# Another order of stages on all engines: score and value products apart on TensorE, the dense head and tail placed anew

## The chip, the cores and the metric

The kernel runs on one core of one Trainium2 chip. The metric is the device time of one launch in microseconds (us), median of three runs.

## The reference

The input is x, 2048 tokens of 128 features. It is layer-normalised to xn, and the output is x + dense(xn) + stack(xn).

- dense(xn): 16-head softmax attention over all 2048 tokens (head width 8, folded projections), then an output product with a bias.
- stack(xn): six layers. Each shifts half of the features by one token, projects to q, k, v (16 heads of 64), normalises each q and k row to unit length, applies gains and rotary tables, attends within a window of 32 tokens and the 32 before (mask, softmax over 64 keys), multiplies by Wo and adds the residual. Then a layer norm, a product up to 2 x 341 columns, a * gelu(gate), a product down to 128 and another residual.

## The kernel before

**Part A** (to about 790 us) is the dense attention: `tensor_a`, `scalar_a`, `vector_a`, `gpsimd_a`, `sync_a`. The change does not touch it. It leaves the unscaled dense result and its row sums in two scratch tensors in DRAM.

**Part B** is the stack: `tensor_b`, `scalar_b`, `vector_b`, `gpsimd_b`, `sync_b`. Its unit of work is a tile of 128 tokens, 16 tiles in each layer, 96 in all. The layer norm and the up and down products work on a chunk of four tiles, 24 chunks in all. Each engine runs one loop `for u in range(FIRST, LAST)`, a round, and a round calls each stage once, for the tile or chunk that is u minus a lag: `score(tile(u - 2))`. `chunk(x)` gives a chunk only for every fourth x. There is no scheduler: an engine works through its list in the order written, and waits at semaphores. The rounds of the engines are not in step; only the semaphores tie them.

The stages of a tile: `high_x` and `low_x` cut the input into two parts (ScalarE, GpSimd); `project(u, 0|1|2)` makes q, k and v, six products of 512 columns each (L1274 to L1276); `squares` (ScalarE, L710) and `square_sums` (VectorE, L982) give the row norms; `rotate_cos` (L1000) and `rotate_sin` (L1011, L1012) multiply out of PSUM; `rotated` (L639) and `normalise` (L647) on GpSimd add and scale; `turn` (L1300) transposes four heads' pairs, `turned_q` and `turned_k` (L732, L741, L744) copy them out; `score` (L1315, L1320) is 2 mask products and 128 recorded small ones; `maxima` (L1031), `exponentials` (L762), `prob_sums` (L1038), `prob_reciprocals` (L1045), `scale_probs` (L601) and `blocks` (L1023) are the softmax and its transpose; SyncE's `move_probs` (L464) and `shift_v` (L455, L456) lay out probabilities and v; `values` (L1337) is 128 recorded small products; `values_out` (L752), `output` (L1349) and `residual_1` (L1055) end the tile.

Each small product is one weight load and one matmul, so score is some 260 instructions of TensorE and values 256, where a projection is 12.

Every product writes to PSUM banks that a table, `BANKS`, fixes for even and odd tiles. A later user of a bank waits until the engine that empties it for the user before has signalled (`wait_free`); `bank_users` repeats TensorE's order to find who that is.

The dense result enters in `load_dense` (SyncE), `dense_norm` (VectorE, L1151: reciprocal of the row sums, then a product), `dense_output` (TensorE L1396, ScalarE L846) and `store_dense`, in four early rounds. It leaves in `load_dense_out`, `final_sum`, `finish` (L1405), `final_add`, `store_out` in late rounds.

Of the kernel before, what the change touches and what calls it, by code (L numbers as in the profile page):

```python
# [16 lines left out]
NT = T // P  # L17
CH = 512
NC = T // CH
# [9 lines left out]
DEPTH = 6  # L29
# [34 lines left out]

END = DEPTH * NT
CHUNKS = DEPTH * NC
FIRST, LAST = 0, END + 15
AHEAD = NT + 2
NPT = 8
NV = 4  # L70
# [29 lines left out]
def tile(x):  # L100
    return x if 0 <= x < END else None


def chunk(x):
    c, r = divmod(x - 3, 4)
    return c if r == 0 and 0 <= c < CHUNKS else None


def early(x):
    return x if 0 <= x < NC else None  # L110


def late(x):
    c = chunk(x)
    return c if c is not None and c >= CHUNKS - NC else None
# [1 line left out]


BANKS = {"q": ((4, 5), (4, 5)), "k": ((2, 3), (2, 3)), "v": ((0, 1), (4, 5)),
         "q_turn0": ((1,), (6,)), "q_turn1": ((6,), (7,)), "k_turn0": ((6,), (7,)),  # L120
         "k_turn1": ((0,), (1,)), "values": ((2, 3), (2, 3)), "output": ((6,), (6,)),
         "score": ((0, 1), (0, 1)), "mean": ((7,), (7,)), "var": ((4,), (4,)),
         "up0": ((4, 5), (4, 5)), "up1": ((2, 3), (2, 3)), "up2": ((6, 7), (6, 7)),
         "down": ((7,), (7,)), "att": ((7,), (7,)), "finish": ((7,), (7,))}
OUT = {"q": "q_out", "k": "k_out", "v": "v_out", "q_turn0": "qT_out0", "q_turn1": "qT_out1", "k_turn0": "kT_out0", "k_turn1": "kT_out1",
       "values": "oT_out", "output": "y_out", "score": "smexp",
       "mean": "mean_out", "var": "var_out", "up0": "up_out0", "up1": "up_out1", "up2": "up_out2", "down": "down_out", "att": "att_out",
# [3 lines left out]
def bank_users():  # L131

    users, last = {}, {}

    def take(stage, unit):
        if unit is not None:
            of = BANKS[stage][unit % 2]
            users[stage, unit] = [last[b] for b in of if b in last]
            last.update({b: (stage, unit) for b in of})

    for u in range(FIRST, LAST):
        take("att", early(u - 3))
        take("q_turn0", tile(u - 2))
        take("k_turn0", tile(u - 2))
        take("v", tile(u - 1))
        take("up0", chunk(u - 8))
        take("var", chunk(u - 6))
        take("up2", chunk(u - 8))
        take("down", chunk(u - 10))
        take("up1", chunk(u - 8))  # L150
        take("score", tile(u - 2))
        take("values", tile(u - 4))
        take("q", tile(u))
        take("finish", late(u - 11))
        take("output", tile(u - 4))
        take("k", tile(u))
        take("q_turn1", tile(u - 1))
        take("k_turn1", tile(u - 1))
        take("mean", chunk(u - 4))
    return users  # L160


# [247 lines left out]
def sync_b(e, w, m, s, d, out_rows):  # L410
    def load_qkv(n, j):
        c = slice(j * INNER, (j + 1) * INNER)
        w.wait_ge(s[f"proj{j}"], n * NT)
        for k in range(2):
            e.dma_start(m.w_qkv[:, k, c].bitcast(F32), m.cut_dram["Wqkv"][k, n][:, c]).then_inc(s[f"ld_wqkv{j}"], 16)
# [85 lines left out]
    load_w1(0)  # L501
    load_w2(0)
    load_cols(0)
    for x in range(1, END + 14):
        if x < END:
            load_rot(x)
        if early(x - 4) is not None:
            store_dense(x - 4)
        if early(x - 2) is not None:
            load_dense(x - 2)  # L510
        n, i = divmod(x - 1, NT)
        if 0 < n < DEPTH and i == 0:
            load_qkv(n, 2)
        if tile(x - 3) is not None:
            shift_v(x - 3)
        n, i = divmod(x - 4, NT)
        if 0 < n < DEPTH and i == 0:
            load_wo(n)
        if tile(x - 4) is not None:
            move_probs(x - 4)  # L520
        n, i = divmod(x - 0, NT)
        if 0 < n < DEPTH and i == 0:
            load_qkv(n, 0)
        n, i = divmod(x - 9, NT)
        if 0 < n < DEPTH and i == 0:
            load_w2(n)
        n, i = divmod(x - 7, NT)
        if 0 < n < DEPTH and i == 0:
            load_w1(n)
        n, i = divmod(x - 0, NT)  # L530
        if 0 < n < DEPTH and i == 0:
            load_qkv(n, 1)
        n, i = divmod(x, NT)
        if n + 1 < DEPTH and i == NT // 2:
            load_gains(n + 1)
        if 0 < n < DEPTH and i == 0:
            load_cols(n)
        c = late(x - 13)
        if c is not None:
            store_out(c)  # L540
        c = late(x - 9)
        if c is not None:
            load_x(c % NC)
        c = late(x - 8)
        if c is not None:
            load_dense_out(c % NC)
    w.wait_ge(s["st_out"], 16 * NC)


# [36 lines left out]
def gpsimd_b(e, w, m, s):  # L586
# [64 lines left out]
    for i in range(2):  # L651
        e.memset(m.k_T[i][:, :, 0:WIN], 0.0).then_inc(s["zeroB"], 1)
    for u in range(FIRST, LAST):
        rotary(tile(u - 1))
        scale_probs(tile(u - 4))
        rotated(tile(u - 2), 0)
        rotated(tile(u - 2), 1)
        root_slope(tile(u - 2))
        root_fix(tile(u - 2))
        normalise(tile(u - 2), 0)  # L660
        normalise(tile(u - 2), 1)
        low_x(tile(u))

# [38 lines left out]
def scalar_b(e, w, m, s):  # L702
# [145 lines left out]
    e.preload_act_table_set("natural_log_exp_and_others")  # L848
    wait_part_a(w, s)
    for u in range(FIRST, LAST):  # L850
        root_estimate(tile(u - 3))
        values_out(tile(u - 6))
        exponentials(tile(u - 4))
        squares(tile(u - 2), 0)
        turned_q(tile(u - 3), 1)
        turned_k(tile(u - 3), 1)
        squares(tile(u - 2), 1)
        deviation_squares(chunk(u - 7))
        dense_output(early(u - 4))
        turned_k(tile(u - 3), 0)  # L860
        turned_q(tile(u - 3), 0)
        keep_v(tile(u - 2))
        ln_root_estimate(chunk(u - 7))
        high_x(tile(u))
        high_ln(chunk(u - 8))
        gelu_table(chunk(u - 9))
        gelu(chunk(u - 9), 0)
        gelu(chunk(u - 9), 1)
        scale_shift(chunk(u - 8))
        gelu(chunk(u - 9), 2)  # L870
        root_table(chunk(u - 9))

# [99 lines left out]
def vector_b(e, w, m, s):  # L972
# [184 lines left out]
    e.tensor_copy(m.mask_bf[:, :, :, :], m.lnb[:, 0:4 * WIN].rearrange("p (a b) -> p a b", a=2).unsqueeze(2).to_broadcast(  # L1157
        [P, 2, NP, 2 * WIN])).then_inc(s["mask"], 1)
    for u in range(FIRST, LAST):
        ln_root_fix(chunk(u - 6))  # L1160
        final_add(late(u - 11))
        residual_1(tile(u - 4))
        prob_sums(tile(u - 2))
        rotate_cos(tile(u), 0)
        prob_reciprocals(tile(u - 2))
        rotate_sin(tile(u), 0)
        rotate_cos(tile(u), 1)
        add_epsilon(chunk(u - 5))
        rotate_sin(tile(u), 1)
        dense_norm(early(u - 1))  # L1170
        square_sums(tile(u), 1)
        gated(chunk(u - 7), 0)
        square_sums(tile(u), 0)
        ln_root_slope(chunk(u - 5))
        gated(chunk(u - 7), 1)
        root_argument(tile(u))
        maxima(tile(u - 1))
        low_ln(chunk(u - 6))
        gated(chunk(u - 7), 2)
        first_scale(chunk(u - 5))  # L1180
        residual_2(chunk(u - 10))
        final_sum(late(u - 10))
        deviation(chunk(u - 4))
        blocks(tile(u - 2))

# [84 lines left out]
def tensor_b(e, w, m, s):  # L1270
# [135 lines left out]
        t.then_inc(s["fin_T"], 1)  # L1406

    for u in range(FIRST, LAST):
        dense_output(early(u - 3))
        turn(tile(u - 2), 0, 0)  # L1410
        turn(tile(u - 2), 1, 0)
        project(tile(u - 1), 2)
        up_product(chunk(u - 8), 0)
        variance(chunk(u - 6))
        up_product(chunk(u - 8), 2)
        down_product(chunk(u - 10))
        up_product(chunk(u - 8), 1)
        score(tile(u - 2))
        values(tile(u - 4))
        project(tile(u), 0)  # L1420
        finish(late(u - 11))
        output(tile(u - 4))
        project(tile(u), 1)
        turn(tile(u - 1), 0, 1)
        turn(tile(u - 1), 1, 1)
        mean(chunk(u - 4))


def build(nc, d, out):
# [59 lines left out]
```

## Time and profile before

| | us |
|---|---|
| median of 3 runs | 2557.55 |
| lowest and highest run | 2550.57, 2572.85 |
| the profiled execution, its own time | 2566.67 |
| its span, first to last instruction | 2564.8 |
| TensorE busy in the span | 2224.1 (87%) |
| VectorE, ScalarE, GpSimd busy | 2038.6, 1765.5, 1307.7 |
| mean granted TensorE clock | 0.928 of full |

The part of interest is the stretch from 823 us (the first score product) to 2500 us. Busy time is what an engine's instructions cover. A wait is idle time, put down to the instruction whose end released it; "issue" is idle time that nothing in the profile explains.

### The profile page before, as it was taken

To read this page: it belongs to the slowest core of one execution; us is meant where nothing else is said; L and a number is where in the kernel's file an instruction comes from. 1 tells how busy PE (TensorE), PEld (TensorE's weight loads), DVE (VectorE), ACT (ScalarE), POOL (GpSimd) and SP (SyncE) were. 2 spreads that over 40 slices of the span, in tenths; PEclk is the share of its full clock that TensorE was granted. 3 is DMA by queue.
4 is the path that set the end of the run, shared out by engine and by line. 5 is a ranking of instruction groups with operands and counts; after the bars stand their busy time and mean duration, and the time that the engine had idled before them with its cause. 6 is when DMAs were issued, how large, how long until landed. Compare 5 with 4: busy or idle time off the path is not lost. (4 is left out here: it accounts for less than half of the span.)

```text
span 2564.8 us, 82297 instructions
## 1 busy us (share of the span) xinstructions
PE 2224.1 (87%) x34487; PEld 1379.1 (54%) x34487; DVE 2038.6 (79%) x2417; ACT 1765.5 (69%) x4192; POOL 1307.7 (51%) x1085
## 2 busy tenths in 40 slices
PE   5899999999996788888888888888989888888986
PEld 3122222222223566676776767677767767667764
DVE  6999989989953878777877778787888788788873
ACT  1277878878774667776776767676777777677762
POOL 4111111111003667777776767666776667677750
PEclk8599999999998889999998989998999999999997
DMA  1213222312112322433233323423243323433321
GB/s 39 82 50 89 61 79 61 89 49 65 36 63 54 90 74 70 118 83 76 75 78 105 82 76 76 118 74 87 76 117 80 84 66 76 117 76 88 84 71 47
DMA packets 167464, 197.61 MB, mean 77 GB/s; under 512 B 87479, under 2 KB 105141, under 8 KB 167093
## 3 DMA queue, kind: packets, MB, share of 16 engines
q1 hardware_dynamic: 166740, 192.14, 28.4%
q8 instruction: 272, 4.46, 0.7%
q14 instruction: 100, 0.81, 0.1%
q10 hardware_dynamic: 352, 0.20, 0.1%
HBM read 57.83 MB, written 27.26 MB: 33 GB/s over the span
## 5 line engine op out<-in xcount | busy, mean ns | idle before, releaser
L699 ACT ACTIVATE PT<-E_ps 128x512 f32<-128x512 f32 x1024 | 534.4, 602 | 196.6 <-PE E_ps L1242 195.1
L938 DVE TENSOR_REDUCE mx<-S_ps 128x1 f32<-128x1024 f32 x512 | 601.5, 1218 | 37.1 <-PE S_ps L1233 31.4
L639 POOL TENSOR_TENSOR tc<-tc,ts 128x1024 f32<-128x1024 f32 x192 | 453.8, 2379 | 9.5 <-DVE ts L1012 9.3
L647 POOL TENSOR_TENSOR tc<-tc,rs 128x1024 f32<-128x1024 f32 x192 | 371.6, 1956 | 13.8
L1233 PE MATMUL S_ps<-KS,QS 48*128 48x512 bf16 x1024 | 330.7, 408 | 31.0 <-DVE mx L938 22.0
L601 POOL TENSOR_TENSOR pr<-pr,mxB 128x1024 f32<-128x1024 f32 x96 | 184.4, 1920 | 310.6 <-DVE mxB L1045 310.6
L1274 PE MATMUL B_ps<-w_qkv,x_cut 128*128 128x512 f32 x576 | 276.7, 480 | 68.4 <-DVE ts L1012 58.0
L1242 PE MATMUL E_ps<-QS,KS 64*128 64x512 bf16 x1024 | 321.8, 391 | 4.7 <-ACT PT L699 4.6
L762 ACT ACTIVATE pr<-B_ps,mxB 128x64 f32<-128x64 f32 x1536 | 324.0, 372 | 0.7 <-DVE mxB L1031 0.7
L581 POOL CAST w_cut_b<-w_raw_b 128x512 fp32r<-128x512 f32 (+1 forms) x48 | 27.6, 574 | 558.4 <-DMA w_raw_b<-in_Wqkv 418.1
L1337 PE MATMUL B_ps<-xy,vs 64*64 64x32 f32 x6144 | 217.7, 226 | 80.9 <-issue 73.1
L1250 PE MATMUL O_ps<-PT,va 128*32 128x512 f32 x2048 | 283.3, 626 | 0.0
L1337 PE MATMUL B_ps<-xy,v 64*64 64x32 f32 x6144 | 219.1, 226 | 67.6 <-issue 67.5
L1055 DVE TENSOR_TENSOR stream<-B_ps,stream 64x128 f32<-64x128 f32 x96 | 27.2, 283 | 309.2 <-PE B_ps L1349 309.1
L1242 PEld LDWEIGHTS E_ps<-QS,KS 64*128 64x128 bf16 x1024 | 79.3, 95 | 326.0 <-ACT PT L699 232.3
L1000 DVE TENSOR_TENSOR tc<-B_ps,rt 128x1024 f32<-128x1024 f32 x192 | 234.1, 1219 | 17.3 <-POOL rt L614 7.6
L1276 PE MATMUL B_ps<-w_qkv,x_cut 128*128 128x512 f32 x576 | 246.5, 428 | 0.6 <-issue 0.6
L1275 PE MATMUL B_ps<-w_qkv,x_cut 128*128 128x512 f32 x576 | 246.6, 428 | 0.2 <-issue 0.2
L1337 PEld LDWEIGHTS B_ps<-xy,vs 64*64 64x64 f32 x6144 | 191.4, 141 | 95.5 <-issue 83.5
L1337 PEld LDWEIGHTS B_ps<-xy,v 64*64 64x64 f32 x6144 | 195.3, 142 | 72.5 <-issue 72.5
L982 DVE TENSOR_REDUCE ss<-nrm 128x16 f32<-128x1024 f32 x192 | 225.9, 1208 | 0.0
L752 ACT ACTIVATE o_T<-B_ps 128x1024 f32<-128x1024 f32 x96 | 98.3, 1024 | 181.6 <-PE B_ps L1337 181.6
(191 smaller groups left out, 4354.0 us busy)
## 6 DMA issues: line engine op xcount, KB each, us to landing
xy<-pc SPq DMA_DIRECT2D x768, 64.0 KB, 2.1
vs<-v SPq DMA_DIRECT2D x96, 384.0 KB, 3.6
Wqkv_cut<-w_cut_b SPq DMA_DIRECT2D x72, 256.0 KB, 2.4
w_qkv<-Wqkv_cut SPq DMA_DIRECT2D x36, 512.0 KB, 5.1
rot<-in_rot SPq DMA_DIRECT2D x96, 128.0 KB, 2.6
vs<-v SPq DMA_DIRECT2D x96, 128.0 KB, 3.7
w_raw_b<-in_Wqkv SPq DMA_DIRECT2D x36, 256.0 KB, 3.1
W_cut<-w_cut_b SPq DMA_DIRECT2D x24, 170.5 KB, 2.6
```

The source lines that it names most:

```text
L639: e.tensor_tensor(tc[:, :], tc[:, :], m.ts[i][:, :], ALU.add).then_inc(s[f"rot{n}"], 1)
L647: e.tensor_tensor(tc, tc, m.rs[u % 2][2][:, i * H:(i + 1) * H].unsqueeze(2).to_broadcast([P, H, DH]), ALU.mult).then_inc(s[f"{n}_scaled"], 1)
L699: e.activation(m.PT[n % NPT][:, :], turns.bank("probs", n)[:, :], ACT.Exp).then_inc(turns.sem("probs", n), 1)
L762: a = e.activation(pb[:, :, h, :], sc[:, h, :, :], ACT.Exp, bias=m.mxB[:, 0, h:h + 1], scale=1.0)
L938: e.tensor_reduce(m.mx[h % 2][:, i, hf:hf + 1], m.S_ps[n % 2][:, :, :], AX.XY, ALU.max).then_inc(s["sc_max"], 1)
L1233: mm = e.matmul(m.S_ps[n % 2][:, c, :], m.QS[sl][rows, i * P:(i + 1) * P], m.KS[sl][rows, k:k + CH], start=True, stop=True)
L1242: e.matmul(turns.bank("probs", n)[:, :], m.KS[sl][rows, j * P:(j + 1) * P], m.QS[sl][rows, chunk_cols(c)], start=True, stop=True).then_inc ...
L1250: e.matmul(m.O_ps[VC * c:VC * (c + 1), :], m.va[:, j, h, :], m.PT[n % NPT][:, :], start=(j == 0), stop=(j == NT - 1)).then_inc(s["pv"], 1)
L1274: e.matmul(bank, left[0], right[0], start=True, stop=False)
L1275: e.matmul(bank, left[0], right[1], start=False, stop=False)
L1276: return e.matmul(bank, left[1], right[0], start=False, stop=True)
L1337: mm = e.matmul(bank[at, a, j, b, :], v[r, d:d + DH], m.xy[u % 2][r, b, par * NP + j, :], start=(b == j == 0), stop=True, skip_group_check ...
```

## The change

The calls in the round loops of part B come in another order, with other lags, and some PSUM banks are others. No instruction is added or taken out, and no shape is changed. The loops run two more rounds, mostly empty ones.

Counted from the tile that is scored, TensorE's round before was: score, values, q, output, k, the four turns with mean among them, v, and in chunk rounds up 0, var, up 2, down, up 1. It is now: score, q, values, k, output, turn k0, q0, q1, mean, turn k1, v, up 0, up 2, var, down, up 1. The transposed q of the first half goes to bank 4, which is one of q's own two banks; `values` goes to banks 6 and 7, `output` to 7, `down` to 6. `dense_output` comes in rounds 0 to 3 and no longer 3 to 6.

```diff
-         "q_turn0": ((1,), (6,)), "q_turn1": ((6,), (7,)), "k_turn0": ((6,), (7,)),
-         "k_turn1": ((0,), (1,)), "values": ((2, 3), (2, 3)), "output": ((6,), (6,)),
+         "q_turn0": ((4,), (4,)), "q_turn1": ((1,), (5,)), "k_turn0": ((6,), (6,)),
+         "k_turn1": ((0,), (7,)), "values": ((6, 7), (6, 7)), "output": ((7,), (7,)),
...
-         "down": ((7,), (7,)), "att": ((7,), (7,)), "finish": ((7,), (7,))}
+         "down": ((6,), (6,)), "att": ((7,), (5,)), "finish": ((7,), (7,))}
... SyncE (x is its round)
+        if early(x - -1) is not None:
+            load_dense(x - -1)
...
+            load_qkv(n, 0)   # with 1 and 2 in the same round x = 16 n; 2 was at x - 1
... GpSimd
+        low_x(tile(u))
+        scale_probs(tile(u - 3))
+        rotary(tile(u))
+        rotated(tile(u - 1), 1)
+        root_slope(tile(u - 1))
+        root_fix(tile(u - 1))
+        normalise(tile(u - 1), 1)
+        normalise(tile(u - 1), 0)
+        rotated(tile(u), 0)
... ScalarE
+        exponentials(tile(u - 4))
+        squares(tile(u - 2), 1)
+        turned_q(tile(u - 3), 0)
+        turned_q(tile(u - 3), 1)
+        turned_k(tile(u - 3), 0)
+        turned_k(tile(u - 3), 1)
+        keep_v(tile(u - 2))
+        deviation_squares(chunk(u - 6))
+        high_ln(chunk(u - 8))
+        ln_root_estimate(chunk(u - 7))
+        dense_output(early(u - 1))
...
+        root_estimate(tile(u - 2))
+        squares(tile(u - 1), 0)
+        values_out(tile(u - 5))
... VectorE
+        gated(chunk(u - 9), 2)
+        final_sum(late(u - 11))
+        ln_root_slope(chunk(u - 7))
+        maxima(tile(u - 3))
+        rotate_cos(tile(u - 1), 0)
+        square_sums(tile(u - 1), 0)
+        rotate_sin(tile(u - 1), 0)
+        ln_root_fix(chunk(u - 7))
+        residual_1(tile(u - 5))
+        prob_sums(tile(u - 3))
+        low_ln(chunk(u - 8))
+        rotate_cos(tile(u - 1), 1)
+        prob_reciprocals(tile(u - 3))
+        rotate_sin(tile(u - 1), 1)
+        dense_norm(early(u))
...
+        blocks(tile(u - 3))
+        residual_2(chunk(u - 10))
+        first_scale(chunk(u - 6))
... TensorE
-        dense_output(early(u - 3))
-        turn(tile(u - 2), 0, 0)
-        turn(tile(u - 2), 1, 0)
-        project(tile(u - 1), 2)
-        up_product(chunk(u - 8), 0)
...
-        score(tile(u - 2))
-        values(tile(u - 4))
-        project(tile(u), 0)
-        finish(late(u - 11))
-        output(tile(u - 4))
-        project(tile(u), 1)
...
+        score(tile(u - 3))
+        finish(late(u - 12))
+        project(tile(u - 1), 0)
+        values(tile(u - 5))
+        project(tile(u - 1), 1)
+        output(tile(u - 5))
+        turn(tile(u - 2), 1, 0)
+        turn(tile(u - 2), 0, 0)
+        turn(tile(u - 2), 0, 1)
+        mean(chunk(u - 5))
+        turn(tile(u - 2), 1, 1)
+        project(tile(u - 1), 2)
...
+        down_product(chunk(u - 10))
+        dense_output(early(u))
+        up_product(chunk(u - 8), 1)
```

## Rows read from the trace of the kernel before

**Rows 1.** Busy time by stretch: columns are named in its first line.

```profile
core 0: us, PE busy (x) PEld busy (x) DVE busy (x) ACT busy (x) POOL busy (x), PEclk, DMA share, GB/s
823.00:2500.00 1677.00, 1449.24 (x29848) 1156.19 (x29848) 1323.89 (x1672) 1189.53 (x3102) 1178.12 (x945) 0.94 0.33 85
...
1853.50:1856.90 3.40, 3.40 (x11) 2.84 (x11) 1.09 (x1) 3.40 (x15) 3.26 (x3) 0.50 0.62 176
```

**Rows 2.** First and last mask products, two a tile, 96 tiles: start times.

```profile
L1315 PE MATMUL B_ps<-mask_bf,ident_bf x192: 376/379/650, 822.2 to 2492.0; 128*128 128x512 bf16 x192
```

**Rows 3.** Waits from 823 to 2500 us: waiter <- releaser: total, times, longest.

```profile
PEld B_ps L1337 <- issue: 153.9, 99, 4.2
PE B_ps L1337 <- issue: 140.6, 87, 4.1
...
PE B_ps L1274 <- DVE ts L1012: 53.1, 46, 1.7
```

**Rows 4.** Timeline of TensorE, a round with a stall: start, length, idle before.

```profile
1847.81 0.60 PE L1315 MATMUL B_ps<-mask_bf,ident_bf 128*128 128x512 bf16 x2
1848.35 1.49 PE L1320 MATMUL B_ps<-k_T,q_T 64*32 64x64 f32 x128
1849.76 0.32 PE L1337 MATMUL B_ps<-xy,vs 64*64 64x32 f32 x8
...
1850.83 0.28 PE L1337 MATMUL B_ps<-xy,v 64*64 64x32 f32 x5
1852.37 0.24 PE L1337 MATMUL B_ps<-xy,v 64*64 64x32 f32 x2 [1.26 <-issue]
...
1853.31 0.62 PE L1274 MATMUL B_ps<-w_qkv,x_cut 128*128 128x512 f32 x1
```

**Rows 5.** Timeline of TensorE, the round before it, without a stall.

```profile
1833.92 0.60 PE L1315 MATMUL B_ps<-mask_bf,ident_bf 128*128 128x512 bf16 x2
1834.45 1.49 PE L1320 MATMUL B_ps<-k_T,q_T 64*32 64x64 f32 x128
1837.86 0.50 PE L1274 MATMUL B_ps<-w_qkv,x_cut 128*128 128x512 f32 x1
...
1839.77 1.95 PE L1349 MATMUL B_ps<-o_T,w_o 128*128 128x128 f32 x16
1841.47 0.48 PE L1274 MATMUL B_ps<-w_qkv,x_cut 128*128 128x512 f32 x1
...
1842.96 1.03 PE L1300 MATMUL B_ps<-ident,tc 128*128 128x128 f32 x8
...
1846.31 0.50 PE L1274 MATMUL B_ps<-w_qkv,x_cut 128*128 128x512 f32 x1 [0.58 <-DVE ts L1012]
```

**Rows 6.** DMA queues, 823 to 2500 us: packets, MB, share of 16 engines.

```profile
q8 instruction: 235, 3.85, 1.0%
```

**Rows 7.** Timeline of TensorE and SyncE where a layer's weights are loaded.

```profile
1630.80 2.02 SPq L415 DMA_DIRECT2D w_qkv<-Wqkv_cut  x4
...
1640.34 0.32 PE L1337 MATMUL B_ps<-xy,vs 64*64 64x32 f32 x2 [3.81 <-issue]
```

**Rows 8.** Timeline of ScalarE in the round of Rows 5.

```profile
1838.00 1.03 ACT L752 ACTIVATE o_T<-B_ps 128x1024 f32<-128x1024 f32 x1 [0.57 <-PE B_ps L1337]
1838.92 3.38 ACT L762 ACTIVATE pr<-B_ps,mxB 128x64 f32<-128x64 f32 x16
1842.06 1.15 ACT L710 ACTIVATE nrm<-B_ps 128x1024 f32<-128x1024 f32 x1
1843.59 0.60 ACT L732 ACTIVATE q_T<-B_ps 128x512 f32<-128x512 f32 x1 [0.38 <-PE B_ps L1300]
1844.08 0.59 ACT L741 ACTIVATE k_T<-B_ps 128x512 f32<-128x512 f32 x1
1844.56 0.37 ACT L744 ACTIVATE k_T<-B_ps,carry 128x128 f32<-128x128 f32 x1
1844.81 1.04 ACT L710 ACTIVATE nrm<-B_ps 128x1024 f32<-128x1024 f32 x1
```

**Rows 9.** Groups of VectorE instructions: busy, mean ns.

```profile
L1000 DVE TENSOR_TENSOR tc<-B_ps,rt 128x1024 f32<-128x1024 f32 x188 | 229.2, 1219 | 3.6 <-ACT nrm L710 0.8
L982 DVE TENSOR_REDUCE ss<-nrm 128x16 f32<-128x1024 f32 x190 | 223.6, 1208 | 0.0
L1011 DVE TENSOR_TENSOR ts<-B_ps,rt 128x512 f32<-128x512 f32 x188 | 129.8, 691 | 8.5 <-DVE tc L1000 0.9 <-issue 0.3
```

**Rows 10.** Timeline at the head of part B, and at the first dense normalisation.

```profile
793.93 0.77 PE L1274 MATMUL B_ps<-w_qkv,x_cut 128*128 128x512 f32 x1 [6.12 <-ACT x_cut L782]
...
802.83 1.22 DVE L1000 TENSOR_TENSOR tc<-B_ps,rt 128x1024 f32<-128x1024 f32 x1 [7.64 <-POOL rt L614]
...
822.47 3.34 DVE L1151 RECIPROCAL hid<-hid 128x512 f32<-128x512 f32 x1
825.84 0.69 DVE L1153 TENSOR_TENSOR hid<-hid 128x512 f32<-128x512 f32 x1
...
802.24 0.43 SPq L445 DMA_DIRECT2D cols<-in_b  x1
...
835.62 1.92 PE L1396 MATMUL B_ps<-hid,w_out 128*128 128x512 f32 x2
```

More of the change, by code:

```diff
@@ L66 @@
 CHUNKS = DEPTH * NC
-FIRST, LAST = 0, END + 15
+FIRST, LAST = 0, END + 17
 AHEAD = NT + 2
@@ L141, in bank_users @@
     for u in range(FIRST, LAST):
-        take("att", early(u - 3))
+        take("score", tile(u - 3))
+        take("finish", late(u - 12))
+        take("q", tile(u - 1))
+        take("values", tile(u - 5))
+        take("k", tile(u - 1))
+        take("output", tile(u - 5))
+        take("k_turn0", tile(u - 2))
         take("q_turn0", tile(u - 2))
-        take("k_turn0", tile(u - 2))
+        take("q_turn1", tile(u - 2))
+        take("mean", chunk(u - 5))
+        take("k_turn1", tile(u - 2))
         take("v", tile(u - 1))
         take("up0", chunk(u - 8))
+        take("up2", chunk(u - 8))
         take("var", chunk(u - 6))
-        take("up2", chunk(u - 8))
         take("down", chunk(u - 10))
+        take("att", early(u))
         take("up1", chunk(u - 8))
[L151 to L159, printed above, removed]
     return users
@@ L503, in sync_b @@
     load_cols(0)
-    for x in range(1, END + 14):
-        if x < END:
+    for x in range(min(0, -1), END + 12):
+        if 0 < x < END:
             load_rot(x)
[L507 to L511, printed above, removed]
+        n, i = divmod(x - 0, NT)
         if 0 < n < DEPTH and i == 0:
-            load_qkv(n, 2)
+            load_qkv(n, 0)
         if tile(x - 3) is not None:
             shift_v(x - 3)
+        if early(x - -1) is not None:
+            load_dense(x - -1)
+        c = late(x - 8)
+        if c is not None:
+            load_x(c % NC)
         n, i = divmod(x - 4, NT)
@@ L518, in sync_b @@
             load_wo(n)
[L519 to L523, printed above, removed]
         n, i = divmod(x - 9, NT)
@@ L526, in sync_b @@
             load_w2(n)
+        c = late(x - 11)
+        if c is not None:
+            store_out(c)
+        n, i = divmod(x - 0, NT)
+        if 0 < n < DEPTH and i == 0:
+            load_qkv(n, 1)
         n, i = divmod(x - 7, NT)
@@ L529, in sync_b @@
             load_w1(n)
+        c = late(x - 7)
+        if c is not None:
+            load_dense_out(c % NC)
         n, i = divmod(x - 0, NT)
         if 0 < n < DEPTH and i == 0:
-            load_qkv(n, 1)
+            load_qkv(n, 2)
+        if early(x - 0) is not None:
+            store_dense(x - 0)
+        if tile(x - 3) is not None:
+            move_probs(x - 3)
         n, i = divmod(x, NT)
-        if n + 1 < DEPTH and i == NT // 2:
+        if 0 <= n < DEPTH - 1 and i == NT // 2:
             load_gains(n + 1)
@@ L537, in sync_b @@
             load_cols(n)
[L538 to L546, printed above, removed]
     w.wait_ge(s["st_out"], 16 * NC)
@@ L653, in gpsimd_b @@
     for u in range(FIRST, LAST):
[L654 to L661, printed above, removed]
-        low_x(tile(u))
+        low_x(tile(u))
+        scale_probs(tile(u - 3))
[6 more added lines that the diff above has]
+        rotated(tile(u), 0)
 def scalar_a(e, w, m, s, d):
@@ L850, in scalar_b @@
     for u in range(FIRST, LAST):
-        root_estimate(tile(u - 3))
-        values_out(tile(u - 6))
         exponentials(tile(u - 4))
-        squares(tile(u - 2), 0)
+        squares(tile(u - 2), 1)
+        turned_q(tile(u - 3), 0)
         turned_q(tile(u - 3), 1)
+        turned_k(tile(u - 3), 0)
         turned_k(tile(u - 3), 1)
[L857 to L861, printed above, removed]
         keep_v(tile(u - 2))
+        deviation_squares(chunk(u - 6))
+        high_ln(chunk(u - 8))
         ln_root_estimate(chunk(u - 7))
-        high_x(tile(u))
-        high_ln(chunk(u - 8))
+        dense_output(early(u - 1))
         gelu_table(chunk(u - 9))
         gelu(chunk(u - 9), 0)
+        high_x(tile(u))
         gelu(chunk(u - 9), 1)
-        scale_shift(chunk(u - 8))
         gelu(chunk(u - 9), 2)
         root_table(chunk(u - 9))
+        scale_shift(chunk(u - 8))
+        root_estimate(tile(u - 2))
+        squares(tile(u - 1), 0)
+        values_out(tile(u - 5))
 def vector_a(e, w, m, s):
@@ L1159, in vector_b @@
     for u in range(FIRST, LAST):
-        ln_root_fix(chunk(u - 6))
-        final_add(late(u - 11))
[L1162 to L1180, printed above, removed]
+        gated(chunk(u - 9), 2)
[13 more added lines that the diff above has]
+        dense_norm(early(u))
+        final_add(late(u - 11))
+        square_sums(tile(u - 1), 1)
+        root_argument(tile(u - 1))
+        gated(chunk(u - 8), 0)
+        gated(chunk(u - 8), 1)
+        deviation(chunk(u - 5))
+        add_epsilon(chunk(u - 6))
+        blocks(tile(u - 3))
         residual_2(chunk(u - 10))
-        final_sum(late(u - 10))
-        deviation(chunk(u - 4))
-        blocks(tile(u - 2))
+        first_scale(chunk(u - 6))
 def tensor_a(e, w, m, s):
@@ L1408, in tensor_b @@
     for u in range(FIRST, LAST):
-        dense_output(early(u - 3))
+        score(tile(u - 3))
[5 more added lines that the diff above has]
+        turn(tile(u - 2), 1, 0)
         turn(tile(u - 2), 0, 0)
-        turn(tile(u - 2), 1, 0)
+        turn(tile(u - 2), 0, 1)
+        mean(chunk(u - 5))
+        turn(tile(u - 2), 1, 1)
         project(tile(u - 1), 2)
         up_product(chunk(u - 8), 0)
+        up_product(chunk(u - 8), 2)
         variance(chunk(u - 6))
-        up_product(chunk(u - 8), 2)
         down_product(chunk(u - 10))
+        dense_output(early(u))
         up_product(chunk(u - 8), 1)
-        score(tile(u - 2))
-        values(tile(u - 4))
-        project(tile(u), 0)
-        finish(late(u - 11))
-        output(tile(u - 4))
-        project(tile(u), 1)
-        turn(tile(u - 1), 0, 1)
-        turn(tile(u - 1), 1, 1)
-        mean(chunk(u - 4))
 def build(nc, d, out):
```

## The prediction

> **What bounds the kernel now.** I read the busy time by stretch, then the list of waits, then the timelines of single rounds. From the first score product to 2500 us TensorE is busy 1449 of 1677 us, 86%; VectorE 1324, ScalarE 1190 and GpSimd 1178 [rows 1]. The 96 tiles follow each other at (2492.0 - 822.2) / 95 = 17.58 us [rows 2]. So TensorE bounds, with 228 us idle. The waits say where: in the value products it sits idle 141 us in 87 rounds (its weight loads 154 us in 99) for "issue", nothing that the profile names [rows 3]. The next largest wait, v's projection for VectorE's `rotate_sin`, is 53 us [rows 3].
>
> What that idle time is can be read from one round. Score runs from 1848.35 and values from 1849.76; after some 80 of 128 value products nothing happens for 1.26 us, in the midst of a run of instructions without a semaphore between them [rows 4]. The round before passes without [rows 5]. Instructions arrive on a queue of their own: 235 packets and 3.85 MB for 2 x 29848 TensorE instructions [rows 6, 1], that is 16 KB and 254 instructions a packet. I read the stall as this: score and values are 516 instructions in 3.8 us (0.54 mask, 1.41 score, 1.85 or so values [rows 4]), and the packet that must follow isn't there. The longest stall, 3.81 us, comes while a layer's weights are under way [rows 7], which fits a late packet.
>
> **The sum, against the profiled execution's 2566.7 us** (9 us above the median, so differences are taken from 2557.55 for the end).
>
> 1. **q's projection between score and values.** It is 12 instructions in 1.4 to 1.5 us (1837.86 to 1839.3 [rows 5], the rest an issue gap). How long a packet takes no row shows; it is bounded: a packet's worth of instructions in the burst runs out in 1.4 us (score) to 1.95 us (values with a hand-over), and the mean stall is 154 / 95 = 1.62 us [rows 3], so the time from the start of one packet to the use of the next is about 3.3 us, an estimate. With q in between, the 256 instructions after a packet boundary in score last 2.7 to 3.2 us, and the stall left is 0.1 to 0.6 us. Boundaries at the start of score, or in the first few products of values, still find a whole burst behind them (about one round in eight, some 1.6 us). Mean left: 0.65 us, 62 us in all. **-92 us.** Bounds: 0 (it isn't instructions at all) and -154.
>
> 2. **The clock.** In 823 to 2500 us it is at 0.94 of full [rows 1], so about 12% of the time at 1.2 GHz. Such a stretch follows the stall of [rows 4]: 3.4 us at 0.50 [rows 1], in which a projection of six products starts them 0.43 apart (1.4 us become 2.6). At 1.2 us per 3.4, 200 us cost at most 70 us. Shorter stalls should spare some: **-15 us**, between 0 (the new order has gaps of its own) and -50.
>
> 3. **values behind q.** ScalarE's chain begins when values end: o_T 0.92, exponentials 3.14, k's squares 0.95, then the four turned halves 0.49 + 0.49 + 0.73 + 0.73 [rows 8], with hand-overs 7.9 us, then the next score. From score's start to the end of values is now 0.54 + 1.41 + 1.5 + 1.85 = 5.3. A round cannot be shorter than 13.2 us. TensorE's own work in a round without chunk products is about 12.2 us (1833.92 to 1847.81 is 13.9 [rows 5, 4], less 0.9 mean, 0.58 and 0.25 of waits). The stall-free round before was 13.9, so the chain costs nothing against it, but it becomes the bound there. In chunk rounds the 3.5 to 4.2 us of up, or var and down, cover it. **0**, bounds -20 and +50 us (1 us in 48 rounds).
>
> 4. **v's wait for `rotate_sin`** (53 us [rows 3]). q now ends 7 us ahead of v, where it was 5.3 us plus the wait. VectorE needs 1.22 + 1.2 + 1.3 [rows 9] after ScalarE's 1.1: gone. But `q_turn0` now lies in q's bank 4, and stands 5.6 us behind q (values 1.95, k 1.45, output 1.75, one turn 0.5); its need is 0.15 + 1.1 + 3.7 + 0.15 = 5.1 us. VectorE has 13.8 us of work a round (1324 / 96), so it is sometimes late; I let this new wait eat the gain, **0**, bounds -45 and +60 us. The stalls' going leaves VectorE at 84% of a 16.5 us round.
>
> 5. **The head.** `dense_output(0)` now stands ahead of the first projection. Its loads follow the columns' (802.7 [rows 10]), some 3.8 us with landing, then 3.34 + 0.69 us on VectorE and 1.92 us on TensorE [rows 10]: q(0) starts at about 812 instead of 793.9; the first rotation, at 802.8 before, comes at about 816, 13 us late. The next rounds each hold a 4 us normalisation in their chain, and rounds 3 to 6 of before are rid of theirs. **+8 us**, bounds 0 and +20.
>
> 6. **SyncE and the tail.** All six w_qkv loads (0.5 MB each; four of them went out in 2.0 us [rows 7]) come in one round. The third pair waits for v of the last tile; behind it is `move_probs`, whose transposes end later, and its values are two rounds off: covered. Without that cover its wait would be v's. Boundary stalls like 3.81 us [rows 7] stay, five of them. `load_dense_out`, `store_out` and `final_add` wait for `finish`, one round on; their followers are late by 2 to 3 us in one full round. Tail: the same chain. **0**, bounds -10 and +15.
>
> Sum: -92 - 15 + 8 = -99; 2566.7 - 99 = 2468, and against the median 2557.55 - 99 = **2458 us**.
>
> The Trainium skill (Runtime: NRT & Kernel Launch, Instruction fetch mechanics) also has fetches of 16 KB blocks, 256 instructions, which the packets bear out. But it says that fetching is hidden, because the sequencer issues more slowly than the memory is filled; by it part 1 would be 0 and the sum -7. That rule is rival B.
>
> **Rivals.**
>
> A. *The stall goes altogether, and the clock's drops with most of it.* For: a stall is cut to zero as soon as a packet takes under 2.7 us. Against: mean stalls of 1.62 say it takes longer. -154 - 28 + 8 = -174: 2384 us.
>
> B. *No change*: the idle time isn't for want of instructions, or each burst of 256 still outruns its packet and stalls by itself, or the gain turns into ScalarE's chain. For: no row shows a fetch waited for. Against: score alone hardly ever stalls, nothing else in these rounds does, and weights under way make it worse [rows 7]. -7 to +15: 2560 us.
>
> C. *Slower: bank 4.* TensorE's `turn(q, 0)` waits for VectorE's `rotate_sin` of the q just projected. It decides once VectorE begins `rotate_cos` over 0.5 us late. `maxima` and, in chunk rounds, the slope and a gate now stand just ahead of it (1.2 to 2.9 us), and `blocks` waits for GpSimd before that. TensorE then stands still, GpSimd's `normalise` gets q late and the next turn too. At 1.9 us late each round: 96 x 1.9 = +182 on -99: 2640 us; it is slower by 1% from 1.3 us a round.
>
> **Chances.** Forecast (2430 to 2500) 0.52, A 0.18, B 0.16, C 0.14. Faster by over 1%: 0.70; within 1% (about what a measurement of this kernel tells from no change): 0.16; slower: 0.14. Range: from A's 2384 to 2570, which takes in B and leaves out C and the far side of A; the likeliest case's own is 2430 to 2500.
>
> **What would show it.** Part 1: the issue wait on L1337 at about 60 us where it was 154, in a gap inside values, and L1320 no worse. Part 2: clock at 0.96 or more. Part 3: rounds without chunk work at 13.5 to 14.5 us, with a small wait of TensorE's mask products for k_T or q_T. Part 4: L1274's wait for ts gone; a wait of L1300 for ts under 20 us. Part 5: first mask product near 835 to 842 us. The prediction fails if L1337's issue wait stays above 120 us, or if L1300 waits for ts over 100 us.

## The result

The changed kernel takes 2410.83 us, median of four runs (2408.15 to 2413.91), beside 2557.66 for the kernel before (four runs, 2550.57 to 2572.85). The ratio is 0.9406, 95% interval 0.9368 to 0.9444. Forecast were 2458 us and -99 us; measured are -147 us. The range, 2384 to 2570, holds it; it lies between the likeliest case and rival A.

The busy time by stretch, first score to shortly before the last, answers [rows 1]:

```profile
core 0: us, PE busy (x) PEld busy (x) DVE busy (x) ACT busy (x) POOL busy (x), PEclk, DMA share, GB/s
823.00:2350.00 1527.00, 1409.62 (x30007) 1113.49 (x30006) 1294.18 (x1684) 1189.12 (x3119) 1181.85 (x950) 0.97 0.36 93
```

TensorE is busy 92% where it was 86%, VectorE 85%. The two stretches do not hold quite the same work; from the first mask product to the last they do (the line of the kernel before stands first):

```profile
822.16:2491.97 1669.81, 1444.79 (x29588) 1151.72 (x29588) 1320.49 (x1668) 1187.77 (x3094) 1178.40 (x945) 0.94 0.33 85
834.07:2332.10 1498.03, 1392.17 (x29582) 1099.27 (x29581) 1273.90 (x1660) 1178.88 (x3091) 1173.47 (x944) 0.98 0.37 94
```

TensorE's idle time went from 225 to 106 us, and its busy time from 1445 to 1392 us for the same instructions, with the granted clock at 0.98 of full where it was 0.94.

The first and last mask products answer [rows 2], and the waits [rows 3]. PE stands for TensorE's products and PEld for its weight loads:

```profile
L1315 PE MATMUL B_ps<-mask_bf,ident_bf x192: 376/377/634, 834.1 to 2332.1; 128*128 128x512 bf16 x192
```

```profile
PEld B_ps L1337 <- issue: 82.9, 141, 3.4
...
PEld B_ps L1320 <- issue: 57.6, 104, 5.3
...
PE B_ps L1337 <- issue: 37.1, 39, 3.3
PE B_ps L1320 <- issue: 14.9, 8, 5.2
PE B_ps L1315 <- ACT k_T L744: 9.3, 23, 0.4
PE B_ps L1300 <- DVE ts L1012: 8.9, 4, 3.0
PE B_ps L1274 <- ACT q_T L732: 6.4, 21, 0.3
```

The issue wait of the value products fell from 141 us in 87 gaps to 37 us in 39 gaps. Their weight loads show 154 and 83 us, but in 141 gaps now: with values behind wide products, weight loads also pause where the products don't stop. So the stops are read from PE. 15 us of them now lie in score (1 us before). v's wait for `rotate_sin`, 53 us, is gone from the list, and what came new is small. One round on TensorE's timeline, to be held against [rows 4]:

```profile
1700.62 0.60 PE L1315 MATMUL B_ps<-mask_bf,ident_bf 128*128 128x512 bf16 x2
1701.15 1.48 PE L1320 MATMUL B_ps<-k_T,q_T 64*32 64x64 f32 x128
1702.56 0.50 PE L1274 MATMUL B_ps<-w_qkv,x_cut 128*128 128x512 f32 x1
...
1704.53 0.28 PE L1337 MATMUL B_ps<-xy,v 64*64 64x32 f32 x2
1705.84 0.25 PE L1337 MATMUL B_ps<-xy,v 64*64 64x32 f32 x3 [1.03 <-issue]
...
1708.98 1.95 PE L1349 MATMUL B_ps<-o_T,w_o 128*128 128x128 f32 x16
1710.77 0.60 PE L1300 MATMUL B_ps<-ident,tc 128*128 128x128 f32 x4
1711.66 1.50 PE L1300 MATMUL B_ps<-ident,tc 128*128 128x128 f32 x12 [0.30 <-DVE ts L1012]
...
1715.44 0.59 PE L1315 MATMUL B_ps<-mask_bf,ident_bf 128*128 128x512 bf16 x2 [0.41 <-ACT k_T L744]
```

The stall still comes in some rounds; this one takes 1.03 us, and the longest, in score, 5.2 us. Two waits that the forecast named stand at their places: 0.30 us of a turn for bank 4, and 0.41 us of the mask product for ScalarE's last copy. Neither grew.

**Where the 147 us are.** Part A, which the change does not touch, ended at different times in the two profiles. VectorE's last copy of the dense result shows it, with the first dense reciprocal of the changed kernel behind:

```profile
775.78 0.69 DVE L965 COPY o_h<-O_ps 128x512 f32<-128x512 f32 x1 [36.18 <-PE O_ps L1250]
...
795.23 3.35 DVE L1151 RECIPROCAL hid<-hid 128x512 f32<-128x512 f32 x1 [12.15 <-DMA hid<-l_scratch]
```

In the profile before, that copy stands at 787.85. (Over all profiles of this study part A ends between 775.7 and 787.9 us.) Of the 158 us between the two profiled executions 12 lie in part A, so part B is what can be compared, from this copy to the span's end:

| profile | copy to first mask product | to last mask product | to the end | part B |
|---|---|---|---|---|
| before | 34.3 | 1669.8 | 72.8 | 1776.9 |
| changed | 58.3 | 1498.0 | 74.3 | 1630.6 |
| difference | +24.0 | -171.8 | +1.5 | -146.3 |

### The profile page after: what moved, and what is told of

Same layout as the page of the kernel before. It is cut to its first block and busy times, and to the rows that moved or that the text cites. A ratio compares the mean times of both kernels' runs of the same rounds, so it can differ in the third digit from the quotient of the medians.

```text
span 2406.4 us, 82195 instructions
## 1 busy us (share of the span) xinstructions
PE 2162.4 (90%) x34487; PEld 1324.6 (55%) x34487; DVE 2003.7 (83%) x2417; ACT 1758.8 (73%) x4192; POOL 1304.7 (54%) x1085
## 5 line engine op out<-in xcount | busy, mean ns | idle before, releaser
L639 POOL TENSOR_TENSOR tc<-tc,ts 128x1024 f32<-128x1024 f32 x192 | 462.5, 2409 | 53.8 <-DVE ts L1012 53.4
L647 POOL TENSOR_TENSOR tc<-tc,rs 128x1024 f32<-128x1024 f32 x192 | 362.3, 1909 | 13.8
L1250 PE MATMUL O_ps<-PT,va 128*32 128x512 f32 x2048 | 276.0, 611 | 0.0
L1274 PE MATMUL B_ps<-w_qkv,x_cut 128*128 128x512 f32 x576 | 262.8, 456 | 10.5 <-ACT q_T L732 6.4
L710 ACT ACTIVATE nrm<-B_ps 128x1024 f32<-128x1024 f32 x192 | 208.4, 1085 | 61.2 <-PE B_ps L1276 59.0
L1275 PE MATMUL B_ps<-w_qkv,x_cut 128*128 128x512 f32 x576 | 233.5, 405 | 1.9 <-issue 1.9
L1276 PE MATMUL B_ps<-w_qkv,x_cut 128*128 128x512 f32 x576 | 233.3, 405 | 2.1 <-issue 2.1
L982 DVE TENSOR_REDUCE ss<-nrm 128x16 f32<-128x1024 f32 x192 | 232.0, 1208 | 0.0
L1337 PE MATMUL B_ps<-xy,vs 64*64 64x32 f32 x6144 | 204.2, 222 | 23.9 <-issue 16.2
L1337 PE MATMUL B_ps<-xy,v 64*64 64x32 f32 x6144 | 204.4, 222 | 21.3 <-issue 20.8
L1337 PEld LDWEIGHTS B_ps<-xy,vs 64*64 64x64 f32 x6144 | 181.4, 137 | 61.4 <-issue 60.7
L1300 PE MATMUL B_ps<-ident,tc 128*128 128x128 f32 x1536 | 198.6, 276 | 15.6 <-DVE ts L1012 8.9
```

What stands on the lines that cost most here:

```text
L639: e.tensor_tensor(tc[:, :], tc[:, :], m.ts[i][:, :], ALU.add).then_inc(s[f"rot{n}"], 1)
L647: e.tensor_tensor(tc, tc, m.rs[u % 2][2][:, i * H:(i + 1) * H].unsqueeze(2).to_broadcast([P, H, DH]), ALU.mult).then_inc(s[f"{n}_scaled"], 1)
L1250: e.matmul(m.O_ps[VC * c:VC * (c + 1), :], m.va[:, j, h, :], m.PT[n % NPT][:, :], start=(j == 0), stop=(j == NT - 1)).then_inc(s["pv"], 1)
L1274: e.matmul(bank, left[0], right[0], start=True, stop=False)
L1275: e.matmul(bank, left[0], right[1], start=False, stop=False)
L1337: mm = e.matmul(bank[at, a, j, b, :], v[r, d:d + DH], m.xy[u % 2][r, b, par * NP + j, :], start=(b == j == 0), stop=True, skip_group_check ...
```

## The experiments

Part B of each is given beside the ratio of its runs to the kernel before. That kernel's own median beside them lay between 2557 and 2573 us, so the ratios, and not the times, are to be compared between experiments. Part B comes from one profile each. Code is cut to the lines that matter, and "..." marks what is left out.

**1. The disputed cost by itself.** `small(n)` issues n fp32 products of 64x64 by 64x32, `wide(n)` n of 512 columns; no semaphore stands inside. (The calls stand one to a line in the kernel, and the signals are left out here.)

```diff
+            wide(12); small(512); wide(12)          # nothing else runs
...
+            wide(12); small(64); wide(12); small(64); wide(1); small(64); wide(2); small(64); wide(4); small(64)
+            wide(12)                                # starts six loads of 1.5 MB
+            wide(4); small(512); wide(4)
```

> The stack is left out: this kernel only copies x to the output and runs TensorE alone, weight load and product in turn, without a semaphore inside a run: 512 small fp32 products of the kind of values (64x64 by 64x32; 1024 recorded pairs), then runs of 64 calls (128 recorded pairs, 256 instructions) with 12, 12, 1, 2 and 4 products of 512 columns ahead of them, then 512 small ones again while 1.5 MB loads run. Theory 1 (instructions come in packets of 16 KB, 256 instructions, some 3.3 us apart): the long run stops every 128 pairs, 1.9 us of work and 1.4 us of idle, 3.3 us a period; with the loads under way the period is 4 us or more; the short runs stop less the longer the products ahead of them last. Theory 2 (the idle time in values comes from something else in the kernel: banks, moved probabilities, vector or scalar engine): the long run goes through at 14.5 ns a pair without a gap, loads or not.

TensorE's timeline, start, length and idle before; a small product is recorded twice, so x128 is 256 instructions:

```profile
7.04 12.73 PE L1461 MATMUL acc<-v,w 128*128 128x512 f32 x24 [7.04 <-DMA x<-in_x]
19.70 3.11 PE L1468 MATMUL acc<-v,w 64*64 64x32 f32 x199
23.76 2.06 PE L1468 MATMUL acc<-v,w 64*64 64x32 f32 x128 [0.95 <-issue]
27.21 2.59 PE L1468 MATMUL acc<-v,w 64*64 64x32 f32 x128 [1.39 <-issue]
31.22 3.63 PE L1468 MATMUL acc<-v,w 64*64 64x32 f32 x128 [1.41 <-issue]
35.22 3.63 PE L1468 MATMUL acc<-v,w 64*64 64x32 f32 x128 [0.37 <-issue]
39.22 8.99 PE L1468 MATMUL acc<-v,w 64*64 64x32 f32 x313 [0.37 <-issue]
...
92.73 1.12 PE L1461 MATMUL acc<-v,w 128*128 128x512 f32 x2
93.79 2.28 PE L1468 MATMUL acc<-v,w 64*64 64x32 f32 x128
...
124.36 2.06 PE L1468 MATMUL acc<-v,w 64*64 64x32 f32 x128 [1.62 <-issue]
130.28 3.63 PE L1468 MATMUL acc<-v,w 64*64 64x32 f32 x128 [3.86 <-issue]
136.48 7.09 PE L1468 MATMUL acc<-v,w 64*64 64x32 f32 x256 [2.56 <-issue]
```

The run stops at every 128 pairs. Starts are 3.5 and 4.0 us apart with nothing else running. When the granted clock falls to 0.50 (31.2 to 48.2 us), 128 pairs take 3.63 us for 2.06, and the stop shrinks from 1.4 to 0.37 us: the period stays at 4.0 us, and the last 313 pairs pass without a stop. So the period belongs to the supply and not to the products. With the loads the periods are 5.9 and 6.2 us, later between 4.0 and 6.2. Rival B's first form (it isn't instructions) falls: there are no banks, no moved data and no other engine here. Runs of 128 pairs with wide calls between them hardly stop, even behind one wide call (2.28 us for 2.06); I had expected graded stops.

The traces show the packets themselves. In this run they start to move at 21.35, 24.87, 28.91, 32.90 and 36.91 us and take 0.92 to 0.96 us; the products go on at 23.76, 27.21, 31.22, 35.22 and 39.22 us, each 1.3 to 1.5 us after the packet's end. It is so in the kernels too. In the round of [rows 4] the packet moves from 1850.18 to 1851.14 us, and the stop ends at 1852.37; the instruction queue in 1850.1 to 1850.3 us:

```profile
q8 instruction: 1, 0.02, 30.0%
```

All 88 issue stops of 0.1 us or more in the value products of the kernel before end 1.2 to 1.6 us after the end of a packet, and so do all 43 of the changed kernel's and its 8 in score. Of the 92 waits for `o_T` in experiment 3 two do. This is the row that the prediction lacked.

**2. Fewer instructions, same order of stages.** Values leaves out the products of the shifted v, and four products of 512 columns ahead of q's take TensorE the same time.

```diff
-            for b, v in enumerate((m.vs[u % 2], m.v[u % NV])):
+            for b, v in ((1, m.v[u % NV]),) if u > 1 else tuple(enumerate((m.vs[u % 2], m.v[u % NV]))):
...
+        if which == 0:
+            for n in range(4):
+                e.matmul(bank[:, 0, :], xc[:, 0, :], m.w_qkv[:, 0, 0:CH], start=True, stop=True)
```

> The same edit in the kernel before: 128 instructions of values left out, four products of 512 columns ahead of q's in their place. Score and values are still adjacent but only 388 instructions. Theory 1: the issue wait in values falls from 154 us to 30 to 70, since no other stage is pushed behind another here. If the pace was TensorE's with its stalls, the time falls by 80 to 120 us, to 2440 to 2480. If VectorE's chain holds it (theory 3), the spared time turns into the wait for rotate_sin (53 us before, 100 or more then) and the gain is under 50 us.

> The changed kernel with the products of the shifted v left out of values from the third tile on (64 recorded products of 128, 128 instructions fewer a tile), and four products of 512 columns repeated ahead of q's, which give TensorE the 0.93 us back. Same work in time, a quarter fewer instructions in the burst. Theory 1: the stalls left there (83 us) are for instructions: they fall under 30, the time by 30 to 60 us to 2350 to 2380. If stalls are cover for something else by now: 2400 to 2415.

In the kernel before: 2465.68 us, ratio 0.9574 (0.9522 to 0.9627), part B 1687.7, 89 us less. Its waits (L1340 is values):

```profile
PE B_ps L1340 <- issue: 88.9, 53, 3.7
...
PE B_ps L1274 <- DVE ts L1012: 42.4, 46, 1.4
```

The issue wait falls by 52 us, less than expected, the wait for `rotate_sin` does not grow (42 us for 53), and the clock in the stack goes from 0.94 to 0.96. The time falls by more than the wait. Not all of that is the stalls' price: here values also ends some 0.9 us sooner in each round, and ScalarE's chain starts with it. In the changed kernel, where q's products stand ahead of values and its end stays in place, the same edit gives 2368.94 us, ratio 0.9196 (0.9153 to 0.9239), part B 1584.9, 46 us less. The products' stops there almost vanish, from 37 to 9 us:

```profile
PEld B_ps L1340 <- issue: 46.2, 99, 2.7
...
PE B_ps L1340 <- issue: 8.9, 6, 2.2
```

**3. The separation alone, in the kernel before.**

```diff
         score(tile(u - 2))
-        values(tile(u - 4))
         project(tile(u), 0)
+        values(tile(u - 4))
```

> The kernel before with one move: q's projection stands between score and values, all else as before. Theory 1: stalls fall by 100 us or so, the slow-clock stretches with them (another 30 to 40), v's wait for rotate_sin (53 us) goes since values now also lies between q and v, and the head's 12 us aren't paid: 2390 to 2440 us. Theory 2: within 1% of 2557.

2562.99 us, ratio 0.9994 (0.9970 to 1.0019), part B 1779.5. I was wrong. The waits of TensorE show why:

```profile
PE B_ps L1349 <- ACT o_T L752: 103.9, 92, 1.3
PE B_ps L1274 <- DVE ts L1012: 62.1, 61, 1.9
PE B_ps L1337 <- issue: 26.5, 32, 2.1
```

The stalls went from 141 to 27 us as theory 1 says. But output now stands directly behind values, and waits 1.1 us in each round for ScalarE's copy. 114 us were spared and 104 paid, and the wait for `rotate_sin` didn't go either (62 us).

**4. Output covered too.** TensorE has the changed order from score to output; the banks had to follow.

```diff
+         "values": ((6, 7), (6, 7)), "output": ((6,), (7,)),
...
+        project(tile(u), 0)
+        values(tile(u - 4))
+        finish(late(u - 11))
+        project(tile(u), 1)
+        output(tile(u - 4))
... VectorE
+        residual_2(chunk(u - 10))     # ahead of residual_1
```

> The kernel before with TensorE in the changed order from score to output: score, q, values, k, output; values in banks 6 and 7, output in 6 or 7 by tile, and VectorE's residual_2 ahead of residual_1, which these banks need. The run with q alone between gave nothing: the instruction stalls in values fell from 154 to 67 us, and output, now right behind values, waited 104 us for ScalarE's copy of o_T. Theory 1 (the separation pays only if something also stands between values and output): the output wait is under 15 us, stalls stay near 70, v's wait for rotate_sin stays at 50 to 70 us, time 2450 to 2490 us. Theory 2 (TensorE's order alone gives nothing, VectorE's and ScalarE's orders set the pace): 2540 to 2570 us, with the 100 us in another wait.

2787.69 us, ratio 1.0896 (1.0840 to 1.0951). The run does not decide what it was made for, since my banks brought waits of their own in chunk rounds: values for `residual_2` and for `deviation`.

```profile
PE B_ps L1337 <- DVE stream L1125: 113.6, 21, 5.5
PE B_ps L1274 <- DVE ts L1012: 94.2, 68, 2.8
PE B_ps L1337 <- DVE xl L1065: 46.3, 22, 3.7
...
PE B_ps L1337 <- issue: 16.3, 21, 1.7
```

What it does show is outside those rounds. From the score of tiles 4n + 1 to the next (only a mean of the chunk's work falls there) it takes 16.6 us, the kernel before 16.2 (means over tiles 12 to 91). The stalls are down to 16 us, the wait for o_T is covered, and the wait for `rotate_sin` grew from 53 to 94 us: the spared time stops there.

**5. The q path first as well** (experiment 4 plus this):

```diff
... ScalarE
+        squares(tile(u - 2), 0)      # ahead of values_out and exponentials
... VectorE
+        rotate_cos(tile(u), 0)
+        rotate_sin(tile(u), 0)       # ahead of residual_1 and prob_sums
```

> e4 with the q path first on the other two engines: ScalarE's squares of q ahead of values_out and the exponentials, VectorE's rotate_cos and rotate_sin of q ahead of residual_1 and prob_sums. v's wait for rotate_sin (53 us before) should fall under 15 us. Theory 1: 30 to 60 us less than e4, 2395 to 2440 us. Theory 2 (the pace is set elsewhere): as e4.

2684.93 us, ratio 1.0494 (1.0446 to 1.0542). The wait for `rotate_sin` is gone from TensorE's list, and tiles 4n + 1 take 14.9 us, where the changed kernel has 14.4. The bank waits stay (111.9 and 47.0 us). Against experiment 4 it is 103 us faster, more than I gave it.

**6. The q path first, alone,** in the kernel before: squares of q ahead of the exponentials, `rotate_cos` and `rotate_sin` ahead of `residual_1`.

> The kernel before, TensorE's order and all banks unchanged, with the q path earlier on the other engines: ScalarE squares q ahead of the exponentials (it was behind them), VectorE does rotate_cos and rotate_sin of q ahead of residual_1 and prob_sums. In the run with q between score and values, and in the one with output covered as well, the spared stalls came back as waits for VectorE's rotate_sin and for o_T. If VectorE's place for the q path is what holds the kernel before (theory 3: the pace is TensorE's time plus a fixed chain to rotate_sin, and both parts of the change are needed): v's wait falls from 53 us to under 10, the time by 30 to 60 us to 2500 to 2530; the issue wait in values stays at 150. If only instruction supply counts (theory 1): 2550 to 2565 us. It can lose: the exponentials start 1 us later, the next score with them.

2625.14 us, ratio 1.0191 (1.0141 to 1.0241), part B 1845.1, 68 us more. VectorE waits for q's squares, and TensorE's stalls in values stay:

```profile
DVE tc L1000 <- ACT nrm L710: 344.5, 168, 7.0
...
PE B_ps L1337 <- issue: 143.3, 85, 3.6
ACT nrm L710 <- PE B_ps L1276: 104.0, 90, 2.0
```

v's wait for `rotate_sin` is gone, as I expected. In its place TensorE's turns wait 43 us for `residual_1` and 28 us for the exponentials, and its mask products 29 us for q_T.

**7. All of the change but the separation.** Values straight behind score; then the same with ScalarE's order made to fit.

```diff
         finish(late(u - 12))
-        project(tile(u - 1), 0)
         values(tile(u - 5))
+        project(tile(u - 1), 0)
... ScalarE, in the second of the two
-        squares(tile(u - 1), 0)
         values_out(tile(u - 5))
+        squares(tile(u - 1), 0)
```

> The changed kernel with values put straight behind score again on TensorE (finish stays between them in three late rounds), all else as changed. Theory 1 (the separation spares instruction stalls): the issue wait in values is back at 1.6 us a tile, the clock falls to 0.93 to 0.95 in the stack, and the time is 2411 + 90 to 130 = 2500 to 2540 us. Theory 2 (the other moves brought the gain): 2405 to 2425 us. Mixed: ScalarE's chain starts 1.45 us earlier, which can give back up to 1 us in the 48 rounds without chunk products.

> The changed kernel with values straight behind score and, other than in the run before it, ScalarE's values_out ahead of q's squares, so that its order follows TensorE's. That run's 2665 us had ScalarE waiting 453 us for q. If instruction stalls are what the separation spares (theory 1): ScalarE's wait for q under 120 us, the issue wait in values at 120 to 170 us against 83 in the changed kernel, output still right behind q with only k... no longer between it and values but q and k both, so no wait for o_T; time 2450 to 2520 us. If only the matching of the two orders counts (theory 2): 2400 to 2425.

2665.54 us, ratio 1.0392 (1.0342 to 1.0442), and 2657.13 us, ratio 1.0383 (1.0333 to 1.0433): both over 100 us above what I expected; part B is 231 and 250 us above the changed kernel's. Waits of the second:

```profile
DVE tc L1000 <- ACT nrm L710: 439.0, 95, 8.6
...
PE B_ps L1300 <- DVE ts L1012: 106.6, 94, 3.0
PE B_ps L1337 <- issue: 80.6, 70, 3.2
...
PE B_ps L1337 <- DVE hid L1111: 36.4, 22, 3.3
```

The stalls are back, but not whole: 81 us in the products, where the changed kernel has 37 and the kernel before 141. They explain 44 of the 250 us. 98 us more come over VectorE: q comes 2 us and a stall later, VectorE has it near the head of its list and waits, and TensorE's turn into bank 4 waits 1.1 us a round for `rotate_sin`. That is rival C's mechanism; its condition is met here and not in the changed kernel. Another 71 us are waits of values for banks 6 and 7 (36 us for `gated`, 19 for `deviation`, 16 for `residual_2`), 5 us in the changed kernel: q's projection between also covers the handing over of banks. So this pair does not measure the stalls alone.

**8. ScalarE's chain shortened** in the changed kernel: exponentials of 8 heads of 16 from the third tile on.

> The changed kernel with the exponentials of 8 heads of 16 left out from the third tile on: 1.6 us a tile less on ScalarE, all else in place. If ScalarE's chain from the end of values to the next score sets the rounds without chunk products (13.2 us by hand, 13.6 to 14 measured), they fall by about 1.2 us to TensorE's own 12.2 to 12.6 and the chunk rounds stay: 48 x 1.2 = 58 us, 2345 to 2360 us. If VectorE or the instruction supply sets them: under 15 us, 2395 to 2411 us.

2389.43 us, ratio 0.9347 (0.9305 to 0.9389), part B 1609.5, 21 us less. 1.6 us a tile bring 0.2. The issue wait of the value products grew from 37 to 48 us, so part of what was spared went there. The chain of 13.2 us binds in few rounds.

**9. The dense head late**, three rounds later (VectorE's part two), in the changed kernel.

```diff
+            store_dense(x - 4)
+            load_dense(x - 2)
... ScalarE, VectorE, TensorE
+        dense_output(early(u - 4))
+        dense_norm(early(u - 2))
+        dense_output(early(u - 3))
```

> The changed kernel with the dense head three rounds later (load_dense at x - 2, normalise at u - 2, product at u - 3, copy at u - 4, store at x - 4), all else as changed. If the head's placing costs what the first score product shows (835.1 against 823.0 us): first score product at 823 to 826 us and 2398 to 2405 us in all, unless the normalisations in rounds 2 to 5 cost in the filling rounds what they spare at the start (then 2411).

2393.09 us, ratio 0.9347 (0.9320 to 0.9374): the fastest kernel of the study that computes everything, though its interval just touches the changed kernel's (0.9368 to 0.9444). Its copy and mask products (this trace has one record of each pair of them, so the first may lie up to half a microsecond earlier):

```profile
784.66 0.69 DVE L965 COPY o_h<-O_ps 128x512 f32<-128x512 f32 x1 [36.18 <-PE O_ps L1250]
```

```profile
L1315 PE MATMUL B_ps<-mask_bf,ident_bf x96: 377/377/634, 819.3 to 2329.1; 128*128 128x512 bf16 x96
```

Copy to first mask product 34.6 us, 23.7 less; then 1509.8 (11.8 more: the reciprocals sit in filled rounds) and 68.5 to the end (5.8 less). Part B 1612.9, 18 us less. The head's new place cost 24 us and gave back 12.

**10. Values in halves**, with k's first half between, on top of experiment 9.

```diff
+        values(tile(u - 5), 0)
+        project(tile(u - 1), 1, (0,))
+        values(tile(u - 5), 1)
+        project(tile(u - 1), 1, (1,))
```

> The fastest kernel so far (dense head late, 2393 us) with values cut in two and k's first half between: score, q, values of heads 0 to 7, first half of k, values of heads 8 to 15, second half of k, output. Stalls in values (82 us) should fall to 30 to 50 us; against that ScalarE's chain starts 0.7 us later and only 0.7 us of k covers o_T's copy of 1.1 us: a wait of 0.4 us at output. A run that shortened ScalarE's chain by 1.6 us a tile gained only 21 us, so 0.7 us more costs 10 to 20. Expected 2380 to 2400 us; over 2410 if the wait for o_T is over 0.8 us a tile.

2464.22 us, ratio 0.9568 (0.9511 to 0.9625), part B 1683.8: 71 us more than experiment 9, where I had expected it faster or the same. Values is L1338, output L1351:

```profile
PEld B_ps L1338 <- issue: 99.6, 215, 3.3
...
PE B_ps L1351 <- ACT o_T L752: 24.3, 83, 2.2
PE B_ps L1338 <- issue: 21.6, 26, 3.2
```

The products' stops did fall, from 36 us in experiment 9 to 22; only the weight loads pause in more places. The wait for o_T is 24 us, 0.25 us a tile, less than expected. From first to last mask product the kernel takes 65 us more (1575 for 1510), and 57 of them are TensorE's busy time (1443 for 1386), for the same number of instructions at the same clock of 0.97; idle time grew by 9 us. So the loss is in no wait. Why the same products take longer when values and k are cut in two stays open.

## Why the prediction was right, and where its sizes were off

- **Part 1, stalls (-92).** Right, in mechanism and size. Stops of the value products fell by 104 us and 14 came new inside score, 90 together. (The sum was made with the weight loads' 154 us; by that measure 71 went.) The time between packets, taken as 3.3 us, is 3.5 to 4.0 in experiment 1. That no row showed a fetch waited for was a gap of the argument, which experiments 1 and 2 and the packets' times close.
- **Part 2, the clock (-15).** Mis-sized: from first to last mask product TensorE's busy time fell by 53 us for the same instructions, past the bound of 50. I tied the clock to the stalls only. The profiles show it with idle time of every kind: in experiment 3 the stops fell by 114 us but the idle time did not (239 us for 225), and the clock went from 0.94 to 0.95 only; experiment 4, with 373 us idle, has 0.91, and the changed kernel, with 106, has 0.98. No run changes the clock by itself, so this is a reading.
- **Part 3, ScalarE's chain (0).** Right: 9 us of mask products waiting for k_T, and experiment 8 finds 21 us in it.
- **Part 4, the two waits for `rotate_sin` (0).** Mis-sized. The old wait went (-53) and the new one at bank 4 took 9 of the 45 that I let it eat. So VectorE does reach q in time. That it does because q stands early in ScalarE's and VectorE's lists fits experiment 5, where moving it there ended the old wait, but in the changed kernel no run tests it.
- **Part 5, the head (+8).** Right in kind; +24 to the first mask product, 12 given back.
- **Part 6 (0).** +1.5 us in the tail. Projections wait 1.6 us in all for a layer's weights (TensorE's group of L1274).
- **The sum** came out 47 us too small, and the time fell outside the likeliest case's 2430 to 2500. Against part B's -146.3: parts 2 and 4 bring 38 and 44 us more than forecast. Against these stand 16 at the head, 1.5 in the tail, 2 in part 1, and some 15 in other waits (k_T 9.3 and q_T 6.4 among them), net of the 12 that the head gave back. The errors partly cancelled. The range holds the time because it reaches down to rival A's 2384 us, and what A says did not happen: to that extent the hit is luck.
- What the prediction didn't see is how the parts hang together. It summed the separation and the order of the q path as if each stood for itself. Alone they give 0 (experiment 3) and +68 (experiment 6), and the change without the separation is 100 us slower than the kernel before (experiment 7). Together they give -172 in the body.
- **Rivals.** A asked that the stalls go altogether: of 142 us of stops 52 are left (37 in values, 15 in score). B falls with experiments 1 and 2 and the packets' times. C's mechanism is real (experiment 7), its condition wasn't met. The Trainium skill's rule that fetching is hidden (Runtime: NRT & Kernel Launch, Instruction fetch mechanics) is not borne out for TensorE's small products: 256 instructions of them take 2.0 us, and the next 256 start 3.5 to 4.0 us after the ones before.

## What to carry to other kernels

A run of some 500 tiny TensorE instructions outruns its own supply here; a stop labelled "issue" in such a run can be told by the packet of instructions that ends shortly before it does. Put a stage of few, long instructions between two such runs, and keep one also ahead of whatever waits for the second run's result. An order of stages pays as a whole: before crediting one move, look in the list of waits for what now stands directly behind what. When profiles are compared, take out the part that the change doesn't touch, since it can differ by 12 us by itself.

## What the runs showed of the hardware that was not expected

- A stop ends 1.2 to 1.6 us after the end of a packet of instructions, in the traces of both kernels and of experiments 1, 2, 3 and 10; a packet's own move takes 0.9 to 1.4 us in experiment 1.
- The first stop of experiment 1 comes after 199 recorded pairs and 24 wide ones, 446 instructions; after that each 256, but for the last 313 pairs, at half clock.
- With loads of 1.5 MB under way 256 instructions take up to 6.2 us to come.
- The granted clock in part A was at half for 82 to 116 us in profiles of the same code, and part A's end moved from 775.7 to 787.9 us with it.
